# Second layer: the convolution's first tap taken out of PSUM by ScalarE, the other taps added by VectorE from SBUF, the backward ones later, and the gates' products moved

## The reference, cut to what matters

```
def _mamba(h, ...):                       # run forward, and on the flipped sequence
    x, z = split(h @ in_proj_W)           # 512 channels each
    x = silu(causal_conv4(x) + conv_b)    # depthwise, 4 taps along the sequence
    xdbl = x @ x_proj_W
    dt = softplus(xdbl[:16] @ dt_proj_W + dt_proj_b); Bm, Cm = the rest of xdbl
    h_t = h_(t-1) * exp(dt_t * A) + dt_t * B_t * x_t      # 32 states per channel
    y = sum over states of h_t * C_t  + Dp * x
    return (y * silu(z)) @ out_proj_W
h = ln(x)*(1+s1)+sh1;  x = x + g1 * (mamba(h) + flip(mamba(flip(h))))
h = ln(x)*(1+s2)+sh2;  x = x + g2 * ((silu(h @ w1) * (h @ w2)) @ w3)     # 384 hidden
```

## Time and profile before

| | |
|---|---|
| median of three runs | 4650.03 us |
| profiled execution, its own time | 4648.52 us |
| its span | 4646.7 us |
| granted clock of TensorE, mean | 0.983 |
| busy: PE, DVE, ACT, POOL | 94%, 89%, 86%, 85% |
| instructions | 81919 |

### The profile page before, as it was taken

How to read it: one execution, slowest core, us unless ns; L and a number is a source line. 1 busy time by engine, 2 the same in 40 slices (tenths; PEclk the granted TensorE clock), 3 DMA queues, 4 the chain that set the end, 5 groups by cost and what they waited for, 6 DMA issues and landing times.

```text
span 4646.7 us, 81919 instructions
## 1 busy us (share of the span) xinstructions
PE 4386.5 (94%) x32260; PEld 3640.8 (78%) x32260; DVE 4144.0 (89%) x4037; ACT 3998.5 (86%) x6263; POOL 3930.1 (85%) x1047
## 2 busy tenths in 40 slices
PE   8989899899899998999999999999999999999998
PEld 4448788788788884458888888888888888888887
DVE  6669999999999986759999999999998999999996
ACT  3459799799889974559999999999999999999995
POOL 4429899889889985539999999999998999999996
PEclk8999999999999999999999999999999999999999
DMA  4001111111111221022242232322321322323221
GB/s 162 1 17 66 58 57 64 54 57 63 56 56 58 67 78 39 1 39 69 74 84 73 88 64 72 84 68 78 84 70 66 84 78 76 76 74 64 76 77 41
DMA packets 241391, 303.40 MB, mean 65 GB/s; under 512 B 116448, under 2 KB 175712, under 8 KB 241008
## 3 DMA queue, kind: packets, MB, share of 16 engines
q1 hardware_dynamic: 241008, 298.15, 22.2%
HBM read 289.84 MB, written 8.26 MB: 64 GB/s over the span
## 4 chain that ended last, share of the span: by engine, by line
PE 45%; ACT 32%; DVE 13%; issue 6%; POOL 4%; DVEq 0%; DMA 0%; SPq 0%; POOLq 0%; ACTq 0%
PE psum L1071 11%; PE psum L1057 9%; PE psum L799 8%; ACT work L1590 8%; ACT work L1609 7%; ACT weights_c L1590 7%; DVE work L2042 6%; PE psum L1054 5%; PE psum L1171 5%; ACT weights_c L1609 4%; DVE weights_c L2042 3%; POOL work L2410 3%; ACT L1372 2%; PE psum L1247 2%; DVE work L1879 1%
## 5 line engine op out<-in xcount | busy, mean ns | idle before, releaser
L2410 POOL TENSOR_TENSOR work<-work,weights_a 128x2048 f32<-128x2048 f32 x512 | 2332.0, 4576 | 242.0 <-DVE work L2042 240.2
L2042 DVE TENSOR_TENSOR_SCAN work<-weights_c,psum 128x512 f32<-128x512 f32 x1366 | 1569.8, 1201 | 93.9 <-PE psum L1057 80.4
L1071 PE MATMUL psum<-ident,work 128*128 128x128 f32 x8192 | 1238.2, 275 | 15.7 <-ACT weights_a L1398 8.1
L2410 POOL TENSOR_TENSOR weights_c<-weights_c,weights_a 128x2048 f32<-128x2048 f32 x256 | 1168.6, 4582 | 57.9 <-DVE weights_c L2042 57.4
L1590 ACT ACTIVATE work<-work,decay 128x504 f32<-128x504 f32 x1366 | 968.3, 709 | 45.8 <-DVE work L2042 22.7
L1071 PEld LDWEIGHTS psum<-ident,work 128*128 128x128 f32 x8192 | 969.0, 142 | 19.9 <-POOL work L2410 10.4
L1057 PE MATMUL psum<-ident,work 128*128 128x128 f32 x5464 | 943.9, 275 | 41.3 <-ACT weights_c L1609 30.4
L2042 DVE TENSOR_TENSOR_SCAN weights_c<-work,psum 128x512 f32<-128x512 f32 x684 | 789.7, 1200 | 30.1 <-PE psum L1057 29.3
L2042 DVE TENSOR_TENSOR_SCAN work<-work,psum 128x512 f32<-128x512 f32 x682 | 786.6, 1199 | 30.7 <-PE psum L1057 18.9
L1057 PEld LDWEIGHTS psum<-ident,work 128*128 128x128 f32 x5464 | 667.9, 142 | 140.5 <-issue 67.3
L1057 PE MATMUL psum<-ident,weights_c 128*128 128x128 f32 x4432 | 771.2, 275 | 0.0
(11 more groups left out here) (192 smaller groups left out, 5785.1 us busy)
## 6 DMA issues: line engine op xcount, KB each, us to landing
weights_a<-c_rows SPq DMA_DIRECT2D x384, 512.0 KB, 3.6
work<-b_diagonals SPq DMA_DIRECT2D x240, 128.0 KB, 2.2
weights_c<-b_diagonals SPq DMA_DIRECT2D x112, 128.0 KB, 2.1
b_diagonals<-weights_c SPq DMA_DIRECT2D x1, 4096.0 KB, 16.3
weights_c<-in_L_cond_fwd_in_w SPq DMA_DIRECT2D x8, 512.0 KB, 5.4
weights_c<-in_L_cond_fwd_xproj_w SPq DMA_DIRECT2D x4, 1024.0 KB, 7.0
weights_c<-in_L_cond_bwd_in_w SPq DMA_DIRECT2D x8, 512.0 KB, 5.3
weights_c<-in_L_cond_bwd_xproj_w SPq DMA_DIRECT2D x4, 1024.0 KB, 7.2
```

Source lines behind the costliest of these rows:

```text
L1071: last = nc.tensor.matmul(PS[:, t, j * P:(j + 1) * P], buf["ring"][s % RING][:, j, t * P:(t + 1) * P], IDENT[:, :], start=begins, stop=((s ...
L2042: v.tensor_tensor_scan(buf["ring"][s % RING][:, j, along], buf["decay"][q % DECAYS][:, along], PS[:, 4 + q % LOOKAHEAD, along], 0.0, ALU.mult,
L2410: g.tensor_tensor(state, state, buf["c"][:, s // 2 % 2, s % 2, :].unsqueeze(1).broadcast_to([P, DC, T]), ALU.mult).then_inc(ss["prod_ready ...
```

## The change

Each chunk's product is now taken out of PSUM by ScalarE, in three instructions (`taps`): a copy into RAW1 in SBUF, and the first tap with weight and bias into XS1 and into XC1. VectorE adds the three shifted taps of XS1 (`conv`) in the three steps after, reading RAW1, and those of XC1 (`back`) one per step, for all chunks after in3. PE's next in product waits for ScalarE's tap in place of the convolution's last addition. The bias is now in the totals, so silu is one instruction of 2048 columns. In runs 3 and 5 the gate products move from before the variance to after in3, and the gaps change. In step numbers after: runs 3 and 5: mean 2, variance 9 and 10, in0 19, in1 24, in2 29, in3 34, gates 38 to 46, bc 53, up 58 to 66, dt3 79, dtx0 98 (before: dt3 81, dtx0 99); run 1: variance 12, in0 25, in1 31, in2 38, in3 44, bc 59, dt3 79, dtx0 95 (before: dt3 81, dtx0 96). The steps of run 7 and of the even runs are as before. In the first attention the places of run -1's pieces are named anew.

```diff
@@ pipe_jobs1
-        jobs += [("mean", KC, 3 if gated or tail and head else 10)]
+        jobs += [("mean", KC, 3 if gated and not first or tail and head else 9)]
...
-    if gated:
-        jobs += [(f"gate{j}", KC, 3) for j in range(HIDDEN1)]
+    gates = [(f"gate{j}", KC, 3) for j in range(HIDDEN1)]
+    if gated and not first:
+        jobs += gates
     if r < RUNS and norms:
-        jobs += [("var", KC, 3 if tail or gated and not first else 16)]
+        jobs += [("var", KC, 3 if tail or gated and not first else 12)]
...
     if first:
-        jobs += [(f"in{j}", KC, 7) for j in range(DC - 1)] + [("in3", KC, 14 if gated else 12), ("bc", DC, 3)]
+        jobs += [(f"in{j}", KC, 5) for j in range(DC - 1)] + [("in3", KC, 3 if gated else 14)]
+        jobs += gates[:-1] + [("gate2", KC, 9)] if gated else []
+        jobs += [("bc", DC, 3)]
@@ PE, beside1
-                            yield from product(f"in{j}", [by("dve", f"conv{j}_7")], chunk(W1["inp"], j), h,
+                            yield from product(f"in{j}", [by("act", f"tap{j}")], chunk(W1["inp"], j), h,
                                                first(lambda: h_made(r)))
+                        if gated:
+                            yield from gates(r - 1)
@@ ScalarE, beside1
                     def silu_x(at, source, ready):
...
-                        for j in range(DC):
-                            last = f(XS1[:, j, :], source[:, j, :], ACT.Silu, bias=vec("L1_cond_conv_b", j))
-                        last.then_inc(done("silu_x"), 1)
+                        ready()
+                        f(XS1, source, ACT.Silu).then_inc(done("silu_x"), 1)
...
+                    def taps(j):
+
+                        yield plan.read(f"in{j}", 2)
+                        made("pe", f"in{j}@{r}")
+                        if r >= 0 and j == 0:
+                            act.wait_ge(ss["skip_added"], r + 1)
+                        col = VCONV + j * 4 + 3
+                        f(RAW1[:, j, :], bank[f"in{j}"], ACT.Copy)
+                        for to in (XS1, XC1):
+                            last = f(to[:, j, :], bank[f"in{j}"], ACT.Identity, bias=vec("L1_cond_conv_b", j),
+                                     scale=VEC[:, col:col + 1])
+                        last.then_inc(done(f"tap{j}"), 1)
@@ ScalarE, first attention
                     behind("square")
+                    ahead("tap1", None)
                     if mlp:
                         square("ln2", LN_A[0], LN_A[1])
-                    ahead(None, "silu_x")
+                    ahead("tap3", "silu_x")
@@ VectorE (convolve before, with its PSUM reads, is gone)
+                def shifted(back, j, shift):
+
+                    col = VCONV + j * 4 + 3 - shift
+                    inside = slice(0, SEQ - shift) if back else slice(shift, SEQ)
+                    x, to = by_sequence(RAW1[:, j, :]), by_sequence((XC1 if back else XS1)[:, j, :])[:, :, inside]
+                    of = x[:, :, shift:SEQ] if back else x[:, :, 0:SEQ - shift]
+                    return v.scalar_tensor_tensor(out=to, in0=of, scalar=VEC[:, col:col + 1], in1=to,
+                                                  op0=ALU.mult, op1=ALU.add)
+
+                def convolve(r, plan, done):
+
+                    for j in range(DC):
+                        for shift in (1, 2, 3):
+                            yield plan.read(f"in{j}", 3 + shift)
+                            made("act", f"tap{j}@{r}")
+                            if shift > 1:
+                                made("dve", f"conv{j}_{shift - 1}@{r}")
+                            shifted(False, j, shift).then_inc(done(f"conv{j}_{shift}"), 1)
+                    for j in range(DC):
+                        for shift in (1, 2, 3):
+                            yield plan.read("in3", 6 + 3 * j + shift)
+                            if shift > 1:
+                                made("dve", f"back{j}_{shift - 1}@{r}")
+                            shifted(True, j, shift).then_inc(done(f"back{j}_{shift}"), 1)
@@ VectorE, first attention
-                        ahead("conv0_7", "in1")
+                        ahead("conv1_1", "in1")
...
-                        ahead("conv1_3", "in3")
+                        ahead("conv2_1", "in3")
```

77 lines of the change are left out of this document (30 added, 47 removed).

## The result

The changed kernel takes 4710.26 us (median of 4 runs, 4706.62 to 4711.03) against 4650.17 us for the kernel before on the same chip (4 runs, 4649.34 to 4651.71): 1.0129 times the time, 95% interval 1.0114 to 1.0144. The prediction was 4705 us. The profiled execution took 4709.96 us with a span of 4708.2 us, 61.5 us more span than before. One profile further down (the first of the two with another order ahead of the first scan) was of an execution at a lower clock (5305.69 us); its trace is not read, only the times of the other three executions.

The account below looks back on a forecast made before the run. No engine total decided; the second layer's VectorE scan pipeline was read in place. Run 5 +20.1, run 3 +20.2, run 1 +14.1, ahead +1 gave +55.4 on 4648.5, 4703.9, median 4705 us; own range 4688 to 4725, wider range 4675 to 4740.

Parts of the forecast that it names:

- Stage A: Scans of a run up to the first convolution: 39.6 us in run 5 (+6.6), 42.8 in run 1 (+6.3).
- The hold: VectorE additions with two SBUF inputs wait until POOL's instruction ends, 0.55 us more: 15.9 us in run 5, 14.5 in run 1.
- no hold: Rival: POOL does not hold these additions; stage B loses 15.9 us twice and 14.5 once, 4659 us; chance 10%.
- half the holds: Rival: POOL holds the additions half the time, as a 2048-column product may let go between parts: 4682 us; chance 13%.
- The tap wait: VectorE waits 2.0 us a chunk for ScalarE's tap, 3.45 at the first: 8.8 us in runs 3 and 5, 8.1 in run 1.
- Stage B: Scans beside the convolution: 75.2 us in run 5 (58.4 before), 77.6 in run 1 (63.7 before).
- The waits in B go: VectorE's waits for PE over the convolution's bank vanish: 4.9 us in run 5, 3.7 in run 3, 1.4 in run 1.
- Stage C: Scans after the convolution: 98.6 us in run 5 (-3.2), 81.2 in run 1 (-6.1).
- their cover: After the convolution, loaded VectorE steps hide the gates' six products at nothing; without that they cost 5 us.
- Ahead: Part worked out in run -1, beside the first attention's last block: +1 us taken, rest of ScalarE order -2 to +3.
- Half rate: Rival: each addition from two SBUF tensors takes 0.67 us more, 72 in the runs +48: 4753 us; chance 6%.
- The faster rival: Rival: tap ready by its slot, norm in time and nothing held; gains 9.4, 10.0 and about 6 us: 4625; chance 6%.

Follow-up runs that it names:

- run 3: Not a follow-up: one of eight runs of 128 VectorE scans in the second layer's pipeline, with convolution; 192.1 us before, 212.0 in the changed kernel.
- run 5: Not a follow-up: one of eight runs of 128 VectorE scans in the second layer's pipeline, with convolution; 193.3 us before, 213.7 in the changed kernel.
- run 1: Not a follow-up: one of eight runs of 128 VectorE scans in the second layer's pipeline, with convolution; 187.5 us before, 202.9 in the changed kernel.
- the schedule alone: Kernel before with gates behind the input chunks and an earlier norm in runs 3 and 5, convolution still VectorE's out of PSUM: 4674.13 us (1.0050).
- the late norm: Changed kernel with mean and variance products of runs 3 and 5 placed later (variance steps 14 and 15, first chunk step 25): 4703.09 us (1.0115).
- the convolution alone: ScalarE's taps and VectorE's 24 SBUF additions as changed, gates and norm where the kernel before has them: 4697.18 us (1.0102).
- the best form of the change: Kernel with the convolution alone, its additions moved behind the third scan of a state, plus three wider gaps: 4667.42 us (1.0039).

## Why the prediction was right, step by step

The total was right to 5 us of a rise of 60, but not every term. Of the 5 us, 4.4 are the stretch ahead of the first scan; in the runs, errors of several us cancel.

- **Stage A**: 39.6 and 42.8 us predicted, 38.6 and 42.8 measured. The wait for "scaled" was given as 5.0 and is 4.78; PE was to wait for "h" 3 us or more and waits 2.82 in run 5 and 4.57 in run 1. The step that GpSimd's chain is unbroken, so that an earlier norm is asked for before it is there, is borne out twice: by the schedule alone (4.84 us) and by the late norm, where that wait went.
- **The hold**: predicted 15.9 us in run 5 and 14.5 in run 1. Measured, over 24 additions at the 0.705 us of the free ones: 35.0 - 16.9 = 18.1 and 36.4 - 16.9 = 19.5. The backward additions came as followed: three holds of 3.2 us a run, 9.5 us for 9.9 or 10.0. The forward ones were undersized: 8.6 us for 6.0 in run 5, 9.9 for 4.5 in run 1. The mechanism taken from one row of L2148 (held to the end of GpSimd's instruction, 0.55 us more) holds within 0.02 us: 0.53, 0.54. Most of the long additions take 3.1 to 3.9 us, though, not the 4 to 5 that I had named as the sign: a scan stands between the start of the product and them. By the Trainium skill (SBUF — State Buffer, "Who interferes with whom") the two engines share a port pair under an exclusive lock; the trace agrees: 36 additions with a PSUM operand (718 ns) and 36 without (1490 ns) in one run. Its rivals, no hold (10%) and half the holds (13%), are out.
- **The tap wait**: this step was wrong. I wrote that VectorE has its first addition three steps after the product; the plan has it four after, since the shifts count from 1. The wait is 0.99 us a chunk and not 2.0 (the first chunk of runs 3 and 5: 4.09, not 3.45), 6.5 us in run 5 for 8.8 and 1.7 in run 1 for 8.1. It is made up for by more holds: with it, the two terms of stage B are 24.6 us in run 5 (24.7 predicted) and 21.2 in run 1 (22.6). That the two trade against each other is seen in the runs (121.1 us together in the changed kernel, 119.8 with the late norm, 121.3 with the convolution alone); that my errors in them cancel so closely is luck, for neither was followed rightly.
- **Stage B** as a whole, 75.2 and 77.6 predicted, has 76.9 and 79.2. "The waits in B go" is where it is short: the waits behind the convolution's bank did go, but VectorE still waits for PE there, 1.93 us in run 5 (behind scan 23) and 3.0 us in run 1 (1.54, 0.83 and 0.68 behind scans 29, 41 and 48), and the sum has nothing for it. TensorE's granted clock alone doesn't explain it: it was 0.91 in this stage of run 5 before and is 0.92, and 0.92 and 0.89 in run 1.
- **Stage C**: 98.6 and 81.2 predicted, 98.2 and 80.9 measured. The terms given add up to -3.0 and -5.3 us, not to the -3.2 and -6.1 that the forecast used; measured are -3.5 and -6.4. PE's wait at dtx0 was to be 3.5 us and is 3.64. The remark that the gates would cost "the 5 us they cost in stage A" if their cover were gone is shown by the schedule alone: 6.2 us in steps 47 to 54.
- **Ahead**: the mis-sized term. I took +1, with +3 at most; it is +5.4. The wait was there (VectorE 1.47 us for ScalarE's tap, the squares 1.5 us later than in the earlier trace rows), but TensorE's idle time grew to 2.72 us and its clock fell behind it, which no term had. The 32 products behind it took 15.74 us and not 14.00. Changing the order alone doesn't cure it.
- **Half rate** (6%): out. By the Trainium skill (Vector Engine (DVE) Microarchitecture Reference, "Points that are easy to get wrong") a scalar_tensor_tensor with two non-bf16 SBUF sources has half the throughput. The free additions here take 0.69 to 0.75 us from SBUF and 0.70 to 0.75 from PSUM, so the measurement decides against it for this form.
- **The faster rival** (6%) needed three things at once; what the best form of the change shows (4667) is that even with most holds at 1.3 us or less they don't come together.

What the forecast didn't say is how the two halves of the change share their costs. It followed both on one timeline, so it needed no price for each; priced one by one they are 24 and 47 us, 60 together, and in run 5 the two together cost under three quarters of their sum.

## What to carry to other kernels

Before moving a VectorE instruction's input from PSUM to SBUF, look whether GpSimd works beside it: with two SBUF tensors it waited in these traces for the end of GpSimd's instruction, whatever its own length, and then the place in GpSimd's rhythm decides (1.95 us or 3.9 us for the same addition). A wait for an engine whose queue is unbroken can move rather than go when one asks for the item at another time: 9.15 us at two places became 7.70 at one. It can also go: with a due step three steps later a hole of 4.06 us was gone as a whole. So a hole in a planned pipeline is worth a look at the due steps before anything is rebuilt: three numbers took 12 us from this kernel, where the rebuilt convolution with its schedule cost 60.

## What the runs showed of the hardware beyond that

- An instruction of 8 columns per partition (0.20 us free) was held 3.3 us by one of GpSimd's like a long one, and ended 0.03 us behind it; the long ones ended 0.52 to 0.55 behind.
- GpSimd is held in turn: its product took 4.87 to 4.97 us when it began 0.47 to 0.56 us before the end of an addition with two SBUF tensors, 4.53 to 4.64 otherwise.
- GpSimd's product of 128x2048 takes 4.58 us; in four pieces of 128x512, 1.28 us each, it takes 4.99 us, some 0.14 us for each further instruction.
- The scans, which read one of their two tensors from PSUM, took 1.19 to 1.22 us each in the second layer, beside GpSimd's products or not: none was held.
- TensorE's granted clock was 0.54 over 5 us (nearly all of it at the lower level, 1.2 of 2.4 GHz) behind an idle time of 2.72 us and 0.51 behind idle times of 0.51 and 1.84 us, but 1.00 behind 1.20 and 1.36 us.
